# Attention and expert block on one core: projection weights in five transfers, value products between the projections, half of the next batch's projections ahead of the score maxima, keys by three transfers instead of six

## The reference

```
qkv = x @ w_qkv                                   # 256 -> 3 * 256, float32
q, k, v = qkv[:, :, 0], qkv[:, :, 1], qkv[:, :, 2]   # 16 heads of 16
q = q / 4
scores = einsum('bqhd,bkhd->bhqk', q, k)          # causal mask, then softmax
attn = softmax(where(mask, scores, -1e10))
out = einsum('bhqk,bkhd->bqhd', attn, v) @ w_out
x = layernorm(x + out)
...                                               # experts, second layernorm
```

## Time and profile before

| | |
|---|---|
| median of 3 runs | 508.43 us (506.52 to 510.31) |
| profiled execution | 509.45 us, span 507.6 us |
| granted TensorE clock, mean | 0.938 |
| PE busy | 410.1 us, 81% |
| DVE, ACT, POOL busy | 57%, 47%, 47% |
| moved by DMA | 72.68 MB, 143 GB/s in the mean |

### The profile page before, as it was taken

How to read it: one execution, slowest core, us unless ns; L and a number is a source line. 1 busy time by engine, 2 the same in 40 slices (tenths; PEclk the granted TensorE clock), 3 DMA queues, 4 the chain that set the end, 5 groups by cost and what they waited for, 6 DMA issues and landing times.

```text
span 507.6 us, 10500 instructions
## 1 busy us (share of the span) xinstructions
PE 410.1 (81%) x3012; PEld 243.6 (48%) x3012; DVE 290.8 (57%) x891; ACT 236.5 (47%) x522; POOL 236.1 (47%) x373
## 2 busy tenths in 40 slices
PE   5767999999987998789845877379888889888892
PEld 2423555555544574345412545146555556556460
DVE  1235846775599859988931665045454445444375
ACT  1411546665556765566622344125444445445242
POOL 4301234323323865288273045744455544544762
PEclk9988999999999999999976997659999999998798
DMA  5786472936671775873832444225545443407592
GB/s 149 171 182 169 109 132 74 175 89 146 188 157 39 149 206 143 189 210 104 239 111 80 106 118 122 104 74 146 155 130 138 133 123 110 120 2 270 211 358 95
DMA packets 51894, 72.68 MB, mean 143 GB/s; under 512 B 9714, under 2 KB 43900, under 8 KB 50304
## 3 DMA queue, kind: packets, MB, share of 16 engines
q1 hardware_dynamic: 44656, 54.83, 43.0%
q0 software_dynamic: 6912, 16.93, 9.1%
q10 hardware_dynamic: 272, 0.26, 0.1%
HBM read 44.24 MB, written 29.66 MB: 146 GB/s over the span
## 4 chain that ended last, share of the span: by engine, by line
PE 54%; DVE 17%; issue 9%; another core or an unknown queue 8%; DMA 5%; ACT 4%; SPq 2%; ACTq 0%; POOL 0%; DVEq 0%
PE PS L646 8%; PE PS L787 7%; PE PS L744 5%; DVE MX L1341 5%; PE PS L766 4%; PE PS L668 4%; PE PS L720 4%; DMA scratch_qk<-PA 3%; PE PS L648 3%; PE PS L731 2%; PE PS L614 2%; PE PS L926 2%; PE PS L748 2%; PE PS L845 2%
## 5 line engine op out<-in xcount | busy, mean ns | idle before, releaser
L1057 ACT ACTIVATE PT<-PS 128x512 f32<-128x512 f32 x160 | 93.0, 596 | 57.6 <-PE PS L766 43.8
L1689 POOL DMA_INDIRECT scratch_y<-Y,XG x80 | 80.0, 1000 | 74.8 <-ACT Y L988 55.0
L1341 DVE TENSOR_REDUCE MX<-PS 128x1 f32<-128x384 f32 (+1 forms) x192 | 88.7, 502 | 36.9 <-PE PS L748 35.1
L1680 POOL DMA_INDIRECT scratch_slots<-XP,RI x64 | 63.2, 988 | 58.7 <-DVE XP L1275 35.1
L1661 POOL TENSOR_SCALAR_AFFINE_SELECT PT<-PT 128x256 f32<-128x256 f32 (+1 forms) x140 | 51.0, 373 | 76.6 <-ACT PT L1057 74.7
L744 PE MATMUL PS<-KS,QS 96*128 96x512 bf16 (+3 forms) x256 | 61.6, 303 | 21.0 <-DVE MX L1341 12.0
L646 PE MATMUL PS<-W,XGT 128*64 x320 | 66.6, 356 | 7.1 <-DVE WG L1196 5.5
L766 PE MATMUL PS<-QS,KS 98*128 98x512 bf16 (+3 forms) x256 | 61.6, 302 | 12.9 <-ACT PT L1057 8.2
L648 PE MATMUL PS<-WG,XGT 128*64 128x192 f32 x320 | 66.7, 356 | 0.0
L1260 DVE SCALAR_TENSOR_TENSOR HH<-PS,XG,SG 128x96 f32<-128x96 f32 x80 | 24.5, 316 | 73.2 <-ACT SG L972 51.9
L668 PE MATMUL PS<-W,HT 96*64 x160 | 44.0, 399 | 15.2 <-ACT HT L979 9.1
(11 more groups left out here) (233 smaller groups left out, 688.6 us busy)
## 6 DMA issues: line engine op xcount, KB each, us to landing
XG<-scratch_slots SPq DMA_DIRECT2D x160, 65.0 KB
scratch_qk<-PA SPq DMA_DIRECT2D x48, 128.0 KB
KS<-scratch_qk SPq DMA_DIRECT2D x48, 128.0 KB, 6.8
W<-_L_ffn_gate_up_proj_dram SPq DMA_DIRECT2D x16, 288.0 KB
YL<-scratch_y SPq DMA_DIRECT2D x8, 512.0 KB, 6.5
QS<-scratch_qk SPq DMA_DIRECT2D x8, 384.0 KB, 5.2
W<-in_L_ffn_down_proj_dram SPq DMA_DIRECT2D x8, 288.0 KB
scratch_slots<-pad SPq DMA_DIRECT2D x17, 130.0 KB, 6.5
```

The costliest lines, as they stand in the source:

```text
L1057: e.activation(PT[:, p % NPT, n, :], PS[:, 2 + (rank[u] - 1) % 2, :], ACT.Exp).then_inc(st_exp, 1)
L1341: t = e.tensor_reduce(M[:, h, qt:qt + 1], PS[:, kk, c0:c0 + w], AX.X, ALU.max)
L1680: e.indirect_dma_start(out=XS[:, :], out_offset=bass.IndirectOffsetOnAxis(ap=RI[:, b % 2, TOPK * q + n:TOPK * q + n + 1], axis=0), in_=XP[ ...
L1689: e.indirect_dma_start(out=YK[:, :], out_offset=bass.IndirectOffsetOnAxis(ap=XG[:, j % NXG, D + 1:D + 2].bitcast(I32), axis=0), in_=Y[:, j ...
```

## The change

Four things change. The weights `w_qkv` come by five transfers (the four blocks of 128 query and key columns, in the order m = 0, 2, 1, 3, then the 256 value columns) instead of one; a projection waits for two of the blocks, the values for theirs. In batch 0 the value products stand between the second and the third projection. In batch 1 the projections m = 0 and m = 2 stand ahead of the first maxima, and `load` 1 stands behind `qkout` (1, 0); the other two projections follow one slot apart from before. In every load the first key part comes by one transfer that reads it three times, and the second by one that reads it twice.

```diff
-            for n, m in enumerate((0, 2, 1, 3)):
+            for m in (0, 2):
                 plan += [(kind, 0, m) for kind in ("qk", "resid", "part", "qkout")]
-                if n == 1:
-                    plan.append(("load", 0))
-            plan += [("v", 0, v) for v in range(2)]
-            plan += [("load", 1)]
+            plan += [("load", 0), ("v", 0, 0), ("v", 0, 1)]
+            for m in (1, 3):
+                plan += [(kind, 0, m) for kind in ("qk", "resid", "part", "qkout")]
...
-            for n, m in enumerate((0, 2, 1, 3)):
-                put(first + 4 * n + 5 * (b > 1), ("qk", b, m))
+            if b == 1:
+                plan += [(kind, b, 0) for kind in ("qk", "resid", "part", "qkout")]
+                plan += [("load", 1), ("qk", b, 2)]
+                put(0, ("resid", b, 2))
+                put(1, ("part", b, 2))
+                put(2, ("qkout", b, 2))
+            for n, m in enumerate((1, 3) if b == 1 else (0, 2, 1, 3)):
+                put(first + 4 * n + (5 if b > 1 else 3), ("qk", b, m))
...
-                    e.dma_start(WQ[:, :, :], w_qkv.rearrange("(c p) n -> p c n", p=128)).then_inc(wq_in, 16)
+                    wt = w_qkv.rearrange("(c p) n -> p c n", p=128)
+                    for m in (0, 2, 1, 3):
+                        e.dma_start(WQ[:, :, 128 * m:128 * m + 128], wt[:, :, 128 * m:128 * m + 128]
+                                    ).then_inc(wq_in[m % 2], 16)
+                    e.dma_start(WQ[:, :, 2 * D:3 * D], wt[:, :, 2 * D:3 * D]).then_inc(wv_in, 16)
...
-                        for p in range(p0, p0 + HD * n, HD):
-                            e.dma_start(KS[r][p:p + HD, :, :],
-                                        SC[1, b, half, part].rearrange("d h t -> d (h t)")).then_inc(ld_in[r], 16)
+                        e.dma_start(KS[r][p0:p0 + HD * n, :, :],
+                                    SC[1, b, half, part].rearrange("d h t -> d (h t)").unsqueeze(0)
+                                    .broadcast_to([n, HD, 8 * S])).then_inc(ld_in[r], 16)
...
-                    e.wait_ge(wq_in, 16)
+                    e.wait_ge(wq_in[m % 2], 32)
...
+                    e.wait_ge(wv_in, 16)
...
-                    e.wait_ge(ld_in[r], 144 * (g // RG + 1))
+                    e.wait_ge(ld_in[r], 96 * (g // RG + 1))
```

More of the change, by code:

```diff
@@ L350, in build @@
         x_in = [sem(f"x_in{b}") for b in range(B)]
-        wq_in, one_in, wo_in, gt_in, spare_in = (sem(n) for n in ("wq_in", "one_in", "wo_in", "gt_in", "spare_in"))
+        wv_in, one_in, wo_in, gt_in, spare_in = (sem(n) for n in ("wv_in", "one_in", "wo_in", "gt_in", "spare_in"))
+        wq_in = [sem(f"wq_in{n}") for n in range(2)]
         w_in = sem("w_in")
```

## The result

The changed kernel takes 561.47 us in the median of 4 runs (557.93 to 562.33), the kernel before 509.37 (506.52 to 511.92): a ratio of 1.1046 (95% interval 1.0986 to 1.1106). The forecast was 535, at most 554. The direction and the mechanism hold; the loss is 52 us where I had 27. The profiled execution took 562.33 us with a span of 560.3, before it was 509.45 and 507.6.

What follows compares the result with a forecast made beforehand. Until 55 us the path through DRAM was taken to bound the kernel, afterwards mostly PE's work. 509.45 us plus 14.9 at the start and 11.8 at later loads gave 536.2 profiled, 535 in the median, range 514 to 554.

Steps and rivals of the forecast that it cites:

- Rival C: Key loads: transfers run on all sixteen engines after all, a set lands at +12.8 us as before; 507 us, chance 0.10.
- D: Later loads: narrow transfers but wholly hidden, only the start counts, at the free rate; +10 us, 518 us, chance 0.18.
- set behind a load, from the QS issue: Sets queued right behind a key load: landing 20.6 us after the QS issue, where it was 12.8.
- end of the remainder of (1, 3): DVE, batch 1: set (1, 2) lands at 61.0 us behind load 1, so this remainder ends at 62.3.
- loads 5 and 6: Later key loads: no set stands behind them, so nothing was counted.
- load 7: Key load with expert weights queued behind: maxima's rows landed at 219.5 us against 217.18, 2.3 us late.
- Price of a load: Key rows of a load: 33 rows on the busiest engines, 8.0 + 5.8 = 13.8 us.
- rival B: Key loads: two of three engines hold each other up at the destination, 2.9 us more a load; 554 us, chance 0.17.
- step 6: 11 `max` steps behind the remainder of (1, 3): 7.3 us, plus 0.5 for negating, ending at 70.1 against 55.22.
- two `max` steps of head start: Later loads: might hide 1 us of each lateness; left out of the sum.
- the sum for loads 2 to 7: Later loads: 2.7, 4.4, 2.4 and 2.3 us late at loads 2, 3, 4 and 7, together 11.8 us.
- A delay before 55 us goes to the end undiminished: Start of the kernel: from 55 us on slots are mostly PE's own work, so an earlier delay stays whole.

Runs made afterwards that it cites:

- run 2: Two kernels: the changed one with key sources read rows outermost (count 16), ratio 1.0043; the one before with six key transfers of outermost count 2, 576.07 us.
- run 3: The changed kernel with the first key part brought by one transfer of two copies and one plain transfer: 548.03 us, ratio 1.0627; the same run as two_engines.
- two_engines: The changed kernel with the first key part brought by a two-copy transfer and a plain one instead of one three-copy transfer: 548.03 us, ratio 1.0627.
- run 5: The changed kernel with one group of expert weights taken up at slot 134 instead of 130: 559.45 us, ratio 1.0976; the same run as weights_later.
- kept_busy: The changed kernel with 50 useless matmuls ahead of batch 0's first `max` step and 60 ahead of the third: 563.23 us, ratio 1.0922.
- six_keys: The changed kernel with the six key transfers of before: 517.54 us, ratio 1.0045.
- weights_later: The changed kernel with one group of expert weights at slot 134 instead of 130, behind the maxima's rows of pairs 24 and 25: 559.45 us, ratio 1.0976.
- narrow_first: The changed kernel with the three narrow key transfers in loads 0 and 1 only, six transfers in loads 2 to 7: 532.58 us, ratio 1.0328.

## Why the prediction was right in kind and half in size

**What held.** What bounds the kernel; that 3 and 2 are the counts by which the transfers are divided (share 0.18 to 0.20, and run 2); QS of load 0 at 15.67 for 15.9; that ACT's copies of (1, 0) and (1, 3) are the places, 1.1 and 2.6 us off; that the other parts are worth little. Rival C, sixteen engines, is out, and so is D.

**Terms that were too small.** The sum was 14.9 + 11.8 = 26.7; it came to 21.8 + 31.9 = 53.7, of which the span shows 52.7. In the table, +22.4 is 22.4 us behind the QS issue of the load.

| term of the prediction | forecast | measured | why |
|---|---|---|---|
| set behind a load, from the QS issue | 20.6 | 21.9, 22.2 | engines collide (run 3) |
| end of the remainder of (1, 3) | 62.3 | 64.94 | two loads of that, less QS 0.2 earlier |
| 11 `max` steps to 76.87 | 7.8 | 11.9 | gate products between them 3.1, clock 0.50 |
| load 2 | 2.7 | 4.5 | set at +22.4 |
| load 3 | 4.4 | 9.3 | keys at +20.3, maxima's rows at +22.8, then the clock |
| load 4 | 2.4 | 6.2 | set at +21.7, then the clock |
| loads 5 and 6 | 0 | 0 and 2.5 | at pair 20, see below; none in two_engines |
| load 7 | 2.3 | 9.1 | keys at +22.4, rows at +26.7, of it 3.3 gone in run 5 |

*Price of a load.* 22.0 - 3.7 - 2.0 - 1.1 = 15.2 us for the key rows instead of 13.8, between my value and rival B's 16.7. I gave B 0.17 and left its 2.9 us wholly out of the forecast; most of it was there. It makes 2.6 us at the start and about 1.5 in each of the later stops.

*Eleven steps.* This is step 6, and the largest miss of the start, 4.1 us. It has three parts. The first six steps, from 64.94 to 69.80, take 4.9 us where the sum had 4.0 and 0.5 for negating. Then DVE waits 3.10 us behind the gate products, which the sum had left out. The last five, from 72.90 to 76.87, take 4.0 instead of 3.3. I priced five steps from 51.90 to 55.22, a stretch that begins just behind the gate products of the kernel before and has clock 1.00 over 4 us:

```profile
49.71 1.87 PE L816 MATMUL PS<-GT,XT 128*128 128x32 f32 x16
```

The stretch ahead of it, 44.0 to 51.5 us, has clock 0.77. The remainder of (1, 1) there is issued at 43.95, and the ten steps behind it take till 55.22, 11.3 us: 1.1 us each, with the gate products and a projection among them. That was about the price that I needed, in a row that I had. At clock 0.50 a score matmul takes 0.61 us instead of 0.38, and the sixteen gate products 3.46 instead of 1.87. Even at full clock throughout they would have been missing from the sum; kept_busy, whose first six steps run nearly all at 1.00, gains 0.3 us there. Seven kernels have 13.54 or 13.55 us from the copy of (1, 3) to p0, whatever stood ahead. It is also why six_keys lost 5.2 us by 60 us, where rival C let it gain. That eleven steps stand behind the remainder and not six is because the projections (1, 1) and (1, 3) stand at slots 3 and 7, where they stood at 8 and 12: five slots earlier, and not one, as the text on the change has it.

*Later loads.* From the QS issue to the operation that waits, before and after: load 2 17.8 and 22.4 us (102.95 - 80.56), load 3 15.5 and 22.8 (138.41 - 115.57), load 4 18.2 and 21.7, load 7 18.5 and 26.7 (269.37 - 242.70). The differences, 4.6, 7.4, 3.6 and 8.2, are stops of PE or ACT; the table has 4.5, 9.3, 6.2 and 9.1. The rest, 1.9, 2.6 and 0.9 us for loads 3, 4 and 7, is lost behind the stop: the granted clock is 0.76 from 139 to 146 us, 0.74 from 168 to 181 and 0.60 from 270 to 277, where the same work before (105 to 111, 128.5 to 139, 217.5 to 224 us) had 1.00, and pair 8 to pair 9 takes 7.31 us instead of 5.61. I counted loads 5 and 6 at nothing because no set stands behind them; from pair 19 to pair 20, behind load 6, it is 8.6 us now and 6.1 before, and 6.1 in two_engines, whose loads are 2 us shorter. PE's timeline has the same two places as at loads 3 and 7, the first scores with the load's keys and the first transposed scores behind them:

```profile
233.83 0.38 PE L755 MATMUL PS<-KS,QS 96*128 96x512 bf16 x1 [1.28 <-DVE MX L1354]
...
235.21 0.38 PE L777 MATMUL PS<-QS,KS 98*128 98x512 bf16 x1 [0.94 <-issue]
```

The first comes 22.9 us behind the QS issue of load 6 at 210.96; before, it came at 190.41, 21.4 us behind, and PE waited at neither. So that load is late by a hair, it seems; the profile puts the first wait down to DVE, and what ended it is not shown. The prediction had no such term, and in loads 3 and 7 it counted the maxima's rows alone and not the keys ahead of them. In load 7, and by the row at 123.44 in load 3 too, SP itself is held (10.36 and 4.69 us), and the maxima's rows are issued late; weights_later shows 3.3 us of it for load 7, together with the weights' bytes. What I named "two `max` steps of head start" hid nothing that can be seen. At load 3 the keys' 20.3 us behind QS are nearly 3.7 + 15.2 + 1.1 = 20.0. I left POOL's scatters out of the sum, and they run then; no run took them away.

**The step that failed** is thus the size of the waits, not their place. The largest is the sum for loads 2 to 7, 11.8 us forecast and 31.9 measured: it priced one wait at each load, and had nothing for the slower stretch behind a stop, for SP being held, or for load 6. Next is step 6, the eleven steps, 7.8 us forecast and 11.9 measured, with the gate products left out and the rows taken at full clock. Last is the price of a load, 20.6 us forecast and 22 measured. "A delay before 55 us goes to the end undiminished" holds in the changed kernel and in narrow_first, but not in six_keys, where part of the 5.2 us is made up later. The upper end of the range, 554, was rival B's value, with the gate products, the slower stretches and the held SP left out as well.

## What to carry to other kernels

Before merging transfers, write down the outermost count of both sides as the DMA sees it: the same bytes in the same three transfers cost 0.4% with 16 outermost and 10% with 3 and 2. And look at what is queued behind a narrow transfer: here ACT waited for the sets, and PE at loads 3 and 7 for the keys and then again for the maxima's rows. When a stretch is priced from rows, take them from the same granted clock that it will have, count in all that PE does within it (here the gate products), and add to every new wait the slow stretch behind it.

## What the runs showed of the hardware that I had not expected

- An issue can hold SP for long while most DMA engines are idle. Behind load 1, WO took 4.78 us and GT 6.63 to issue, behind load 7 one expert weight 10.36; before, WO and GT took 0.48 and 0.49 us. While SP was at GT, the DMA share was 0.19 from 54 to 58 us. WO landed 17.5 us after its issue, before 7.0.
- In kept_busy the granted clock was 1.00 through a wait filled with matmuls of no use and for 4 us more, in which PE was busy for 2.12, and then 0.50 for 8 us, in which PE was busy for 7.54.
- Three engines with 33, 33 and 17 rows are slower than two with 34, by 2.1 to 2.5 us a load, and it is one of the two with 33 that ends late.
